# Attention: the value sums of two steps in one block, paired maximum banks, three single score banks

## What is computed

```python
q = _rms(heads(wq), qn_w); k = _rms(heads(wk), kn_w); v = heads(wv)     # 16 heads of 16
scores = jnp.einsum('bhqd,bhkd->bhqk', q, k) * HD ** (-0.5)
scores = jnp.where(causal[None, None], scores, -jnp.inf)
attn = jax.nn.softmax(scores, axis=-1)
ao = jnp.einsum('bhqk,bhkd->bhqd', attn, v)
```

## Time and profile before

| | us |
|---|---|
| median of 3 runs | 2749.78 (2748.95 to 2756.04) |
| profiled execution, its time | 2751.05 |
| profiled execution, span of its instructions | 2748.9 |
| PE busy / DVE / ACT, of the span | 2500.2 (91%) / 1949.9 (71%) / 1279.7 (47%) |
| attention, first maxima to last sums | 1078.8 to 1990.7 |

### The profile page before, as it was taken

The page is one execution under the profiler, slowest core; times in us unless marked ns, Lnnn a source line. Parts: engine busy times, 40 slices in busy tenths (PEclk is TensorE's granted clock), DMA queues, the critical chain, the costliest instruction groups (busy, mean ns, idle before and its releaser), DMA issues. The chain is left out here.

```text
span 2748.9 us, 67671 instructions
## 1 busy us (share of the span) xinstructions
PE 2500.2 (91%) x26848; PEld 1787.8 (65%) x26848; DVE 1949.9 (71%) x3760; ACT 1279.7 (47%) x1945; POOL 78.4 (3%) x94
## 2 busy tenths in 40 slices
PE   5999888888898984999999999999959999999999
PEld 4777777777777773333333333333249999999998
DVE  6877777777777773987888888888355565656554
ACT  3333333333333320466666666666734445454444
POOL 0000000000000002100000000000060000000000
PEclk9999999999999997999999999999979999999999
DMA  2011000011100001210111101100030101010100
GB/s 73 14 25 25 21 21 21 22 24 26 26 21 21 22 19 53 70 40 24 59 30 38 55 21 50 39 24 13 12 120 23 34 23 36 21 38 19 38 19 27
DMA packets 138282, 90.14 MB, mean 33 GB/s; under 512 B 68544, under 2 KB 130624, under 8 KB 138048
## 3 DMA queue, kind: packets, MB, share of 16 engines
q1 hardware_dynamic: 136448, 81.34, 10.4%
q0 software_dynamic: 1600, 5.24, 0.6%
HBM read 56.89 MB, written 29.36 MB: 31 GB/s over the span
## 5 line engine op out<-in xcount | busy, mean ns | idle before, releaser
L1268 DVE TENSOR_REDUCE a_mx<-a_pm 128x1 f32<-128x512 f32 (+3 forms) x1120 | 709.4, 672 | 146.1 <-PE a_pm L1166 83.9
L1250 ACT ACTIVATE a_pt<-a_sc 128x1024 f32<-128x1024 f32 (+3 forms) x640 | 544.8, 897 | 361.8 <-PE a_sc L1190 189.6
L1166 PE MATMUL a_pm<-a_ka,a_qa 96*128 96x512 bf16 (+3 forms) x1280 | 402.9, 355 | 15.6 <-DMA a_qa<-q_scratch 11.7
L1187 PE MATMUL a_sc<-a_qa,a_ka 98*128 98x512 bf16 (+3 forms) x1280 | 354.5, 349 | 29.8 <-ACT a_pt L1250 18.5
L1166 PEld LDWEIGHTS a_pm<-a_ka,a_qa 96*128 96x128 bf16 x1280 | 123.8, 98 | 306.8 <-DVE a_mx L1268 213.5
L1206 PE MATMUL a_po<-a_pt,a_v_st 128*32 128x512 f32 (+3 forms) x2560 | 300.9, 542 | 0.1
L1793 DVE TENSOR_TENSOR e_h_lo<-v_all,e_h_hi 128x512 fp32r<-128x512 f32 x208 | 146.3, 704 | 189.1 <-ACT e_h_hi L1640 188.0
L1187 PEld LDWEIGHTS a_sc<-a_qa,a_ka 98*128 98x128 bf16 x1280 | 116.7, 98 | 147.7 <-ACT a_pt L1250 58.8
L1638 ACT ACTIVATE v_all<-e_ps 128x512 f32<-128x512 f32 x176 | 103.4, 588 | 125.0 <-PE e_ps L1530 124.3
L1530 PE MATMUL e_ps<-e_h_hi,e_e_l_hi 128*128 128x256 f32 x512 | 147.7, 288 | 0.0
L1530 PE MATMUL e_ps<-e_h_lo,e_e_l_hi 128*128 128x256 f32 x512 | 144.8, 283 | 0.0
(11 more groups left out here) (312 smaller groups left out, 5438.9 us busy)
## 6 DMA issues: line engine op xcount, KB each, us to landing
a_ka<-k_scratch SPq DMA_DIRECT2D x192, 64.0 KB, 2.3
a_qa<-q_scratch SPq DMA_DIRECT2D x192, 64.0 KB, 2.3
o_scratch<-a_o_sb SPq DMA_DIRECT2D x32, 256.0 KB, 2.6
v_all<-o_scratch SPq DMA_DIRECT2D x256, 32.0 KB
q_scratch<-r_q_part SPq DMA_DIRECT2D x192, 32.0 KB, 1.5
k_scratch<-r_k_part SPq DMA_DIRECT2D x192, 32.0 KB, 1.6
r_x_tok<-in_x SPq DMA_DIRECT2D x32, 128.0 KB, 2.1
s_scratch<-r_s_tok SPq DMA_DIRECT2D x32, 128.0 KB, 1.7
```

What stands on the lines that cost most here:

```text
L1166: last = mm(out[:, at_:at_ + width], qa[b][0:NP, qc, h0 + i, 128 * (qt % 4):128 * (qt % 4) + 128], ka[b][0:NP, h0 + i, 512 * kc:512 * kc + ...
L1187: last = mm(sc[x][:, y, off:512], ka[b][:, h, 128 * j:128 * j + 128], qa[b][:, qc, h, off:512], start=True, stop=not diag)
L1250: nc.scalar.activation(pt[x][g % 2][:, :, off:512], sc[x][:, :, off:512], ACT.Exp).then_inc(s_p[x], 1)
L1268: ve.tensor_reduce(mx[:, h0:h0 + heads, qt, kc:kc + 1].rearrange("p h o -> p (h o)"), pm[:, k % RING, 0:heads * width].rearrange("p (h w) ...
```

## The change

1. sums(g-1) and sums(g) stand one behind the other in PE's order, at the end of every odd step. pt becomes four buffers of four heads each, so ACT waits for the sums of four steps ago instead of two.
2. A unit of maxima fills two banks (pm is 2 x 2 banks): both heads of a pair, so that one reduction reads 1024 elements (768 for the width of 384, 512 for that of 128). There are 576 units instead of 1120; entry k waits for the reduction of entry k - 2. The masks of a unit come after all its matmuls. plan's cost per unit is changed accordingly.
3. The score buffers are three single banks, one head each, in turn; score n waits for exponential n - 3. There are 1280 exponentials of at most 512 elements instead of 640 of at most 1024. keep_out stands after the second of them.
4. PE's order in iteration g is scores(g, 3); the first entry; scores(g+1, 0); the middle entries; scores(g+1, 1); the last entry; scores(g+1, 2); and after an odd g the two sums.
5. qa is a ring of four groups instead of two full sets, which makes room for the larger pt. The q operand of group i is loaded when the scores of group i - 4 are done; k is loaded as before. Both have semaphores of their own.

```diff
-RING = 3
+RING = 2
+SC = 3
+QRING = 4
...
-                heads = 512 // width
-                for h in range(0, 4, heads):
-                    yield ("U", it, qc, kc, qt, h, heads, width)
+                if width <= 256:
+                    yield ("U", it, qc, kc, qt, 0, 2, width)
+                else:
+                    for pair in range(2):
+                        yield ("U", it, qc, kc, qt, pair, 1, width)
...
-    cost = lambda e: 0.6 if e[0] == "T" else 0.1 + e[6] * e[7] / 960
+    cost = lambda e: 0.6 if e[0] == "T" else 0.15 + 2 * e[6] * e[7] / 960
...
-        pt = [[sb(f"pt{x}{i}", [128, 2, 512]) for i in range(2)] for x in range(2)]
+        pt = [sb(f"pt{i}", [128, 4, 512]) for i in range(4)]
...
+            def load_qa(it, c):
+
+                i = it * QC + c
+                if i >= QRING:
+                    sp.wait_ge(s_sc, 4 * done(i - QRING))
+                operands(qa[0:NP, i % QRING, :, :], "q", PARTS_Q, it, slice(512 * c, 512 * c + 512), s_qa[i % QRING])
...
+                n = 4 * g + h
+                off = max(0, 128 * (j - 4 * qc))
+                i = it * QC + qc
+                if j == 0 and h == 0:
+                    pe.wait_ge(s_mload[i % QRING], 32 * turns(i))
+                if n >= SC:
+                    pe.wait_ge(s_p, n - SC + 1)
+                diag = j >= 4 * qc
+                last = mm(sc[:, n % SC, off:512], ka[b][:, h, 128 * j:128 * j + 128],
+                          qa[:, i % QRING, h, off:512], start=True, stop=not diag)
...
-            scores(0, 0)
-            scores(0, 1)
+            for h in range(3):
+                scores(0, h)
             for g in range(ITS * NS):
                 ks = in_slot.get(g, [])
-                a, z = (len(ks) + 1) // 3, (len(ks) + 1) // 3 + len(ks) // 2
+                scores(g, 3)
+                maxima(ks[:1])
...
                 if g + 1 < ITS * NS:
                     scores(g + 1, 0)
-                maxima(ks[:a])
+                    maxima(ks[1:len(ks) - 1])
+                    scores(g + 1, 1)
+                maxima(ks[max(1, len(ks) - 1):])
                 if g + 1 < ITS * NS:
-                    scores(g + 1, 1)
-                maxima(ks[a:z])
-                sums(g)
-                maxima(ks[z:])
+                    scores(g + 1, 2)
+                if g % 2:
+                    sums(g - 1)
+                    sums(g)
...
-                if g >= 2:
-                    act.wait_ge(s_pv, g - 1)
-                for x in range(2):
-                    act.wait_ge(s_sc[x], g + 1)
-                    nc.scalar.activation(pt[x][g % 2][:, :, off:512], sc[x][:, :, off:512], ACT.Exp).then_inc(s_p[x], 1)
-                    if j == 0 and g and x == 0:
+                if g >= 4:
+                    act.wait_ge(s_pv, g - 3)
+                for h in range(4):
+                    act.wait_ge(s_sc, 4 * g + h + 1)
+                    nc.scalar.activation(pt[g % 4][:, h, off:512], sc[:, (4 * g + h) % SC, off:512], ACT.Exp
+                                         ).then_inc(s_p, 1)
+                    if j == 0 and g and h == 1:
                         keep_out(it * QC + qc - 1)
...
-                    ve.tensor_reduce(mx[:, h0:h0 + heads, qt, kc:kc + 1].rearrange("p h o -> p (h o)"),
-                                     pm[:, k % RING, 0:heads * width].rearrange("p (h w) -> p h w", h=heads),
+                    heads = mx[:, :, qt, kc] if slots == 2 else mx[:, 2 * pair:2 * pair + 2, qt, kc]
+                    ve.tensor_reduce(heads.rearrange("p (i y) -> p y i", y=2),
+                                     pm[:, k % RING, :, 0:slots * width].rearrange("p y (i w) -> p y i w", i=slots),
                                      axis=AX.X, op=ALU.max).then_inc(s_red, 1)
```

More of the change, by code:

```diff
@@ L1060, in attention_phase, with turns @@
         last_unit = {e[1:3]: k for k, e in enumerate(entries) if e[0] == "U"}
-        s_load = [[sig(f"loaded{b}{c}", 1, 16 * 12).sem for c in range(QC)] for b in range(B)]
-        s_mload = [[sig(f"m_loaded{b}{c}", 1, 16 * 2).sem for c in range(QC)] for b in range(B)]
+        s_ka = [[sig(f"k_loaded{b}{c}", 1, 16 * 6).sem for c in range(QC)] for b in range(B)]
+        s_qa, s_mload = ([sig(f"{n}{i}", 1, 16 * per).sem for i in range(QRING)]
+                         for n, per in (("q_loaded", 6), ("m_loaded", 2)))
+        def turns(i):
+            return i // QRING + 1
         s_ostore = [sig(f"o_stored{c}", 1, 16).sem for c in range(QC)]
@@ L1066, in attention_phase @@
         s_ones, s_kones, s_one = sig("v_ones", 1).sem, sig("k_ones", 1).sem, sig("dve_ones", 1).sem
-        s_sc = [sig(f"scores{x}", 1).sem for x in range(2)]
-        s_p = [sig(f"weights{x}", 1).sem for x in range(2)]
+        s_sc, s_p = sig("scores", 1).sem, sig("weights", 1).sem
         s_pv, s_o = sig("summed", 1).sem, sig("out_kept", 1).sem
@@ L1099, in store, with done @@
                              o_sb[:, c, :]).then_inc(s_ostore[c], 16)
+            def done(i):
+                it, c = divmod(i, QC)
+                return it * NS + FIRST_STEP[c] + 4 * c + 4
             events = []
@@ L1151, in maxima @@
                     e = entries[k]
-                    out = pm[:, k % RING, :]
+                    out = pm[:, k % RING, :, :]
                     if k >= RING:
@@ L1157, in maxima @@
                         pe.wait_ge(s_m, it * QC + qc + 1)
-                        last = nc.tensor.transpose(out[0:16, 0:128], m[:, qc, :], const("ident"))
+                        last = nc.tensor.transpose(out[0:16, 0, 0:128], m[:, qc, :], const("ident"))
                     else:
-                        _, it, qc, kc, qt, h0, heads, width = e
+                        _, it, qc, kc, qt, pair, slots, width = e
                         u, b = divmod(it, B)
-                        if (qt, h0) == (4 * qc, 0) and kc == 0:
-                            pe.wait_ge(s_load[b][qc], 192 * (u + 1))
@@ L1164, in maxima @@
[L1164 to L1170, removed]
-                                          skip_group_check=True)
+                        q_at = (it * QC + qc) % QRING
@@ new lines, in maxima @@
+                        if qt == 4 * qc and kc == 0 and pair == 0:
+                            pe.wait_ge(s_ka[b][qc], 96 * (u + 1))
+                            pe.wait_ge(s_qa[q_at], 96 * turns(it * QC + qc))
+                        for i in range(slots):
+                            for y in range(2):
+                                h = 2 * (pair + i) + y
+                                last = mm(out[:, y, width * i:width * i + width],
+                                          qa[0:NP, q_at, h, 128 * (qt % 4):128 * (qt % 4) + 128],
+                                          ka[b][0:NP, h, 512 * kc:512 * kc + width], start=True, stop=kc != qc,
+                                          skip_group_check=True)
@@ L1172, in maxima, with scores @@
+                        if kc == qc:
+                            for i in range(slots):
+                                for y in range(2):
+                                    last = mm(out[:, y, width * i + width - 128:width * i + width], ident16, neg_qk,
+                                              start=False, stop=True, skip_group_check=True)
                     last.then_inc(s_max, 1)
-            def scores(g, x):
+            def scores(g, h):
                 it, s = divmod(g, NS)
@@ L1178, in scores @@
                 qc, j = STEPS[s]
+                n = 4 * g + h
                 off = max(0, 128 * (j - 4 * qc))
[L1180 to L1187, removed]
-                              qa[b][:, qc, h, off:512], start=True, stop=not diag)
-                    if diag:
-                        last = mm(sc[x][:, y, off:off + 128], ident16, neg_kq, start=False, stop=True)
-                last.then_inc(s_sc[x], 1)
+                i = it * QC + qc
[6 more added lines that the diff above has]
+                          qa[:, i % QRING, h, off:512], start=True, stop=not diag)
+                if diag:
+                    last = mm(sc[:, n % SC, off:off + 128], ident16, neg_kq, start=False, stop=True)
+                last.then_inc(s_sc, 1)
             def sums(g):
```

58 lines of the change are left out of this document (30 added, 28 removed).

## The result

The changed kernel takes 2775.06 us (median of 4 runs, 2773.96 to 2777.43), the kernel before on the same chip 2749.36: a ratio of **1.0093, 95% interval 1.0077 to 1.0109**. It is slower by 26 us; the forecast was 2782. The profiled execution took 2774.86 us with a span of 2773.1.

A forecast was written before the change was run, and what follows sets the result against it. PE was taken to set the pace; longer waits through DVE and ACT would outweigh its saving. 15 + 1 + 7 + 9 = +32 us on 2751.05 gave 2783, as a median 2782; 8-in-10 range 2740 to 2828.

The forecast's parts named there:

- PE's saving: Two sums in one block pay 0.22 us once: 35 us less PE time; a pair by PE alone 5.43, not 5.68.
- rival 3: The pair of sums does not save its gap: 0.22 us more in each chain, 2817 us; chance 0.10.
- rival 1: Neither chain closes, PE sets the pace at 5.43 us per pair: faster, 2710 us; chance 0.16.
- DVE's chain: Ordinary pairs: PE waits for two-bank reductions through the block, 5.95 us instead of 5.68; each further entry adds 1.13.
- Per iteration +2.5: Iterations 1 to 6: pairs with four and five entries, group starts and narrow pairs together add 2.5 us per iteration.
- pairs off the diagonal with four entries: Six pairs of steps per iteration, each 0.27 us longer.
- the same with five entries: Three pairs of steps off the diagonal per iteration, each 0.8 us longer.
- four group starts: Start of each group, where the copy keep_out stalls PE: each gives back about 0.5 us.
- seven narrow pairs: The seven narrow pairs left in each iteration, about 0.1 us longer each.
- Iteration 0, +7: Iteration 0 makes two sets of maxima; its seven heaviest pairs take 61 us instead of 54: +7.
- ACT's chain in the last steps: Last 20 steps, without maxima: a pair takes 5.35 us instead of 4.23, as scores wait for exponentials: +9 us.
- rival 2: A draw: group starts wholly returned and heavy pairs of iteration 0 free, chains 0.08 shorter: 2750 us; chance 0.12.

The follow-up runs named there:

- e9: Single maximum banks and paired sums, with one bank moved from the maxima (three left) to the scores (four): 2769.42 us, 1.0064 of the kernel before.
- e3: The changed kernel with each reduction of maxima reading only the first half of its columns: 2718.26 us.
- e5: The changed kernel with each exponential from step 8 on reading and writing only the first half of its columns: 2766.2 us.
- e1: The changed kernel with the sums made one by one at the end of each step, paired maximum banks kept: 2756.51 us, 1.0024 of the kernel before.
- e2: The changed kernel with four single maximum banks (reductions of 512), sums still paired: 2734.2 us, 0.9934 of the kernel before.
- e4: The changed kernel with four single maximum banks and the sums of each step at its end: 2735.16 us, 0.9946 of the kernel before.
- e6: The changed kernel with the sums of four steps in one block, five weight buffers: 2794.89 us, 1.0150 of the kernel before.
- e7: The changed kernel with four single maximum banks, and single sums in iteration 0 and the last 20 steps: 2720.1 us, 0.9876 of the kernel before.
- e8: Four single maximum banks, single sums made one step later, keep_out behind the fourth exponential, against the changed kernel: 2735.96 us, 0.9921 of the kernel before.

## Why the prediction was right

It went as forecast, slower, at 2775 instead of 2782. Step by step:

- **PE's saving.** Right: 1.85 us from the first load of sums weights to the next load of scores (1.86 forecast), no second gap, so rival 3 is false. No ordinary pair reaches the 5.43: rival 1 is false, since reductions over two banks cost what the extrapolation gave.
- **DVE's chain.** Right in mechanism: forecast 5.95, measured 5.88; e9 shows the coefficient of a bank, e3 and e5 show whose loop it is. The reduction of the first unit starts 1609.93 - 1609.30 = 0.63 after its first matmul (0.64), but the fourth unit follows at 3.05 after it, not 3.13: the 0.10 for a load that nothing covers was counted in full and is not seen in the matmuls' start.
- **Per iteration +2.5: the term that was mis-sized.** Measured +1.57 (111.40 - 109.83); iterations 1 to 5 gave 7.8 us, 12.5 were forecast. Cut PEld's timelines of before and after at the first load behind the sums of each odd step, and every pair of steps has its length. Sorted as in the prediction, in us per iteration, means of iterations 1 to 5:

  | | forecast | measured |
  |---|---|---|
  | pairs off the diagonal with four entries | +1.6 | +0.2 |
  | the same with five entries | +2.4 | +2.6 |
  | four group starts | -2.0 | -1.2 |
  | seven narrow pairs | +0.7 | -0.1 |

  The chain itself held: on the mean of iterations 1 to 5, the 28 pairs with four entries take 5.88 after, the 17 with five 6.97 (7.08 forecast). What failed is the time before: the same pairs with four entries took 5.84 there and not 5.68, because the step of the earlier trace rows is one of the fastest. The pairs with five came as forecast (6.19 before). The errors have opposite signs (the starts against the pairs with four and the narrow ones), so the sum looks better than its terms; that much is luck.
- **Iteration 0, +7.** Measured +5.9 (168.3 - 162.4), and not where it was forecast alone: the seven heaviest pairs went from 54.4 (54 forecast) to 58.8 us (61), +4.4. Another 1.9 came before the end of the first pair, where nothing was forecast, and the rest gave back 0.4. Paired banks with single sums (e1) take 57.4 for the heavy pairs, single banks with paired sums (e2) 57.7, neither (e4) 52.8: here either of the two edits alone costs most of it.
- **ACT's chain in the last steps.** 5.21 against the forecast 5.35; with iterations 6 and 7 together +11.7 (2.5 + 1 + 9 = 12.5 forecast). Of these the last 20 steps are +9.3 (9 forecast), but some 1.5 us are a loss that I had named and not counted, a lower clock (below): the chains alone gave about 8 there, and about 10 in the two iterations.
- **The groups' starts** give back 0.3 us each on the mean (0.5): 0.6 at the first and the third of an iteration, nothing at the second and the fourth, most of which have five entries. The moved q loads cost nothing that the rows show: the long waits of PEld between 1250 and 1750 us name ACT, DVE or issue, not a landing.
- **Outside the attention** nothing was forecast; the recurrent stage was 2.9 us shorter and the rest 1.7 longer in the profiled execution, which says nothing about the change.

Sum: -2.9 + 5.9 + 7.8 + 11.7 + 1.7 = 24.2, the difference of the spans. The draw (rival 2) needed starts and heavy pairs that cost nothing; neither was so.

On DVE's share: by the rows of before its reductions would take 33 us less; its busy time fell by 66. Two reductions of 512 that stand alone take 2 x 0.69 = 1.38 us, one of 1024 takes 1.22: that saves 0.16, more than the 0.06 back to back, and DVE idles between many of them. None of it shortened an ordinary pair, which has 1.27 us of idle DVE.

The Trainium skill (Perfetto Trace Analysis, Optimizing Scalar/DVE Operations) says that where VectorE is not saturated but causes bubbles on other engines, breaking up instructions may let work be completed sooner. The runs agree: with reductions of 512 again, e2 takes 2734 us instead of 2775; it also makes the ring four units deep, and in the same four banks the two can't be separated. The Trainium skill's 125 ns per VectorE instruction on PSUM (same section) gave the prediction 68 us as an estimate, and the busy time agrees with its 66, though back to back only 0.06 us are saved for each two reductions made one.

## What to carry to other kernels

A long block on the producing engine pays only if each ring of buffers between it and a consumer holds work for the block and the hops around it; write the loop down (block, hops, and one consumer distance per entry beyond the ring's depth), and expect each bank moved to change it by one distance (e9 shows it for one bank either way). Four small banks are a deeper ring than two large ones: fewer, larger reductions save the consumer's time and lengthen the loop, and the long block and the shallow ring together cost more than the sum of each. Pair where a stage has slack for it and not where a consumer's loop decides: with four single banks and that rule, +0.9% became -1.2%.

## What was not expected of the hardware

In the last 20 steps of the kernel after, TensorE's granted clock fell once, at their start. Windows of the kernel after:

```profile
1972.00:1974.00 2.00, 1.23 (x16) 0.28 (x5) 0.00 (x0) 1.87 (x5) 0.00 (x0) 1.00 0.10 39
...
1976.00:1977.00 1.00, 1.00 (x5) 0.24 (x9) 0.00 (x0) 1.00 (x3) 0.00 (x0) 0.50 0.00 0
...
1978.00:1979.00 1.00, 1.00 (x8) 0.20 (x4) 0.00 (x0) 0.00 (x0) 0.00 (x0) 0.50 0.00 0
1979.00:1980.00 1.00, 1.00 (x10) 0.15 (x3) 0.00 (x0) 0.00 (x0) 0.00 (x0) 0.82 0.00 0
```

PEld's timeline of the same stretch:

```profile
1976.47 0.20 PEld L1236 LDWEIGHTS a_po<-a_pt,a_v_st 128*32 128x32 f32 x8 [0.44 <-ACT a_pt L1283]
...
1979.73 0.33 PEld L1218 LDWEIGHTS a_sc<-a_qa,a_ka 98*128 98x128 bf16 x3 [1.35 <-issue]
```

From 1973.48 PE had made one score of 512 every 0.49 us, in step with ACT; from about 1976 it was granted 0.50 (the level of 1.2 GHz), and a block of sums lasted 1976.47 to 1979.73 = 3.26 us instead of 1.85. ACT's idle time of 2.81 before 1980.16 is this block. In the pairs behind it, which wait as well, the clock is 1.00. In e2, e3 and e9 it fell in the same way at the start of the last steps (0.50 in 1933 to 1935, 1922 to 1924 and 1989 to 1992), and in e6 three times: 0.50 from 1996 to 2000, with ACT idle for 5.43 us over that block, 0.57 on the mean of 2008 to 2012 and of 2018 to 2026. In the last steps of before, of e1, e4, e5, e7 and e8 the clock is 1.00. So it fell in every kernel that has paired sums or longer blocks there and whole exponentials, and in no other; more is not shown.
